# A gated recurrence in a fused four-layer kernel: head sums moved from VectorE, ScalarE and GpSimd to TensorE, with keys and values dealt to (token, head) partitions by DMA

## The chip, the cores and the metric

The kernel runs on one core of one Trainium2 chip. The metric is the device time of one execution in microseconds (us). The core has five instruction queues: PE (TensorE), DVE (VectorE), ACT (ScalarE), POOL (GpSimd) and SP (SyncE, here only an issuer of DMA transfers). They run side by side and are ordered only by semaphores that the program sets and waits for.

## The reference, cut to what matters

The program computes four residual layers over 8 sequences of 512 tokens with 256 channels. The change lies in the first, a gated recurrence followed by window attention. Of it, this part is touched (`n` sequence, `h` of 8 heads, `e` of 4 recurrences, `t` token, `d` of 64 channels; keys K and values V alike):

```python
G = sigmoid(einsum('ntd,hed->nhet', Xp, w_G) + b_G)
K = einsum('ntc,hdc->nhtd', Xp, w_K)
V = einsum('ntc,hdc->nhtd', Xp, w_V)
A = 1.0 - minimum(G.sum(axis=1), 1.0)
gK = einsum('nhet,nhtd->netd', G, K)
gV = einsum('nhet,nhtd->netd', G, V)
# tokens in 32 pieces of 16; in each piece, from the initial state iK (iV):
# Y[t] = A[t] * Y[t-1] + gK[t]
nK = _pscan(A, gK, iK);  nV = _pscan(A, gV, iV)
```

So each of 4096 tokens has 8 heads of 128 numbers (64 of K, 64 of V). For each `e` the heads are summed with the gates as factors, and the sums run through a linear scan along the tokens.

## The kernel before

The stage `recurrence` works in tiles of 128 tokens, 32 tiles, four to a sequence. Every engine runs one `stream` of steps: the first and last tiles written out, the rest in a hardware loop over sequences, so each engine has its own fixed order and stands still where a semaphore of its next instruction is missing. For a tile:

1. DVE normalises the rows (`normed`, tile `XN`), PE turns them (`turned`, `psT`), ACT copies them to `XT` (L452); SP stores `XT` to DRAM for the window attention (L349).
2. PE makes the gate logits `psG` (L400, L401), ACT takes the exponential (L457), DVE turns it into the gates `G` and the decays `A` in five small instructions (L519 to L529).
3. PE makes keys and values of all heads, tokens on partitions, in two PSUM banks (`psKV`, L409, four products of 512 columns).
4. The head sums are made with per-partition factors, one instruction for each (head, e) pair. Of the 32 pairs of a tile, DVE takes 20 (L542 the first head of an `e`, L545 the others, each adding to `acc`), ACT takes 12 (L470, into `gated`), and POOL adds ACT's twelve up in three instructions (L370, L372, L374).
5. PE turns the sums and the decays so that channels lie on partitions and tokens in a row (`psR`, L418 to L421; `psA`, L425), ACT copies them into `gT` and `AT` (L478, L480).
6. After the fourth tile of a sequence DVE adds the initial state at the first token of each piece of 16 and sets the decay there to zero (L556 to L558), and scans 512 tokens for each of the four `e` (L560), writing `Rec`.

DVE's order in a step: `normed` of the tile four ahead, the 20 pairs with the next tile's gate instructions in between, and, at the first step of a sequence, the scan of the sequence before. PE's order in a step: `turned` of the tile three ahead, gates of the tile two ahead, keys and values of the next tile, sums and decays of the last one. `psKV` has two buffers, so keys and values of a tile wait for the pairs of the tile two before.

The next stage, `window_attention`, starts behind a barrier of all engines, needs `Rec` and the first sequence of `XS`, loaded back from DRAM at the stage's end (L196). Instructions of other stages are not touched.

## Time and profile before

| | |
|---|---|
| median of 3 runs | 2017.03 us (2015.64 to 2017.1) |
| the profiled execution | 2017.16 us |
| its span, first to last instruction | 2015.4 us |
| mean granted TensorE clock | 0.918 |
| PE busy over the span | 1679.7 us (83%) |
| DVE busy over the span | 1211.6 us (60%) |
| ACT, POOL busy over the span | 664.2 us, 592.1 us |

The span is what the prediction works with, and the 1.8 us around it are taken as constant. Shares over the whole span say little here, since the change touches one stage, the first sixth of it. So the rows below are nearly all of that stage. In the rows, "PEld" is a weight load of PE, which runs beside the products. A product of float32 appears as two instructions (L409: 256 instructions for 128 products), a transpose as one. In a timeline a row may merge several neighbouring instructions of a kind (x4): its start is the first one's and its length reaches to the end of the last.

### The profile page before, as it was taken

What the parts mean: (1) busy time and instruction counts of PE and PEld (TensorE: products, weight loads), DVE (VectorE), ACT (ScalarE), POOL (GpSimd) and SP (SyncE); (2) the same over time, 40 slices, a digit from 0 to 9 for tenths busy, and PEclk for the clock granted to TensorE, in tenths of its full rate; (3) what the DMA queues carried; (4) which work ended last, traced back from release to release, by engine and by line L of the source; (5) the groups of instructions that cost most, each with busy time, mean ns of one, the idle gap of its engine ahead of it and who ended that gap; (6) DMA issues with size and microseconds to landing.
All of it is one profiled execution on the core that took longest, in us unless ns stands there. A gap on an engine that the chain in (4) does not pass through costs nothing. (4 is left out here: it accounts for less than half of the span.)

```text
span 2015.4 us, 33318 instructions
## 1 busy us (share of the span) xinstructions
PE 1679.7 (83%) x10092; PEld 1252.5 (62%) x10092; DVE 1211.6 (60%) x3206; ACT 664.2 (33%) x2056; POOL 592.1 (29%) x668
## 2 busy tenths in 40 slices
PE   4777765999899977367786999999599999699999
PEld 2444434777677754256675788888366666455655
DVE  5999994777677767599945122222388888422221
ACT  2545544555455533112230111111144444211121
POOL 2443432000000011587626332332354554100000
PEclk9898987999899998777775899999799999799999
DMA  6000000000000000000011232432210110000000
GB/s 187 17 16 13 16 21 11 12 11 12 13 12 12 1 9 0 6 0 22 21 67 70 86 110 89 94 104 62 94 30 29 31 31 17 1 11 21 10 21 21
DMA packets 55111, 71.08 MB, mean 35 GB/s; under 512 B 7074, under 2 KB 44898, under 8 KB 54626
## 3 DMA queue, kind: packets, MB, share of 16 engines
q1 hardware_dynamic: 37218, 40.46, 6.3%
q0 software_dynamic: 6912, 18.88, 3.6%
q10 hardware_dynamic: 10880, 10.49, 1.5%
q8 instruction: 51, 0.84, 0.2%
q14 instruction: 50, 0.41, 0.1%
HBM read 46.61 MB, written 23.20 MB: 35 GB/s over the span
## 5 line engine op out<-in xcount | busy, mean ns | idle before, releaser
L801 ACT ACTIVATE probs<-psS,nm 128x256 f32<-128x256 f32 x256 | 118.9, 469 | 191.9 <-DVE nm L834 191.9
L409 PE MATMUL psKV<-wkv,XT 128*128 128x512 f32 x256 | 135.4, 678 | 52.2 <-DVE acc L545 32.5
L1576 DVE COPY YE<-e_psY 128x512 f32<-128x512 f32 x40 | 27.6, 691 | 220.6 <-PE e_psY L1522 220.6
L545 DVE SCALAR_TENSOR_TENSOR acc<-psKV,G,acc 128x128 f32<-128x128 f32 x544 | 150.1, 332 | 6.7 <-ACT gated L470 6.7
L1512 PE MATMUL e_psH<-e_XT,w 128*128 128x256 f32 x640 | 147.3, 384 | 0.0
L1522 PE MATMUL e_psY<-w,e_HT 128*128 128x256 f32 x640 | 144.0, 379 | 0.0
L832 DVE TENSOR_REDUCE mx<-psS 128x2 f32<-128x512 f32 x128 | 87.8, 686 | 93.4 <-PE psS L722 93.4
L722 PE MATMUL psS<-Rec,QT 128*128 128x256 f32 (+1 forms) x512 | 134.4, 385 | 6.8 <-issue 5.9
L1482 POOL DMA_INDIRECT XE<-token_rows,held x80 | 76.0, 950 | 200.0 <-PE e_psX L1499 180.3
L1522 PEld LDWEIGHTS e_psY<-w,e_HT 128*128 128x128 f32 x640 | 121.6, 190 | 16.5
L1512 PEld LDWEIGHTS e_psH<-e_XT,w 128*128 128x128 f32 x640 | 120.7, 193 | 15.4
L1552 ACT ACTIVATE e_HT<-e_psH 128x512 f32<-128x512 f32 x80 | 47.8, 597 | 234.1 <-PE e_psH L1512 212.9
L409 PEld LDWEIGHTS psKV<-wkv,XT 128*128 128x128 f32 x256 | 52.6, 217 | 112.0 <-issue 94.6
L470 ACT ACTIVATE gated<-psKV,G 128x128 f32<-128x128 f32 x384 | 103.8, 407 | 36.0 <-DVE acc L545 18.3
L1104 PE MATMUL o_psA<-ident,prodV 128*128 128x128 f32 x400 | 61.6, 318 | 59.9 <-POOL prodV L1043 59.9
L722 PEld LDWEIGHTS psS<-Rec,QT 128*128 128x128 f32 x512 | 94.7, 192 | 21.5 <-issue 9.9
L2223 DVE SCALAR_TENSOR_TENSOR f_HT<-f_psU,f_SG 128x512 f32<-128x512 f32 x48 | 33.2, 692 | 124.2 <-PE f_psU L2155 111.1
L666 POOL COPY R<-Rec 128x2176 f32 (+1 forms) x8 | 16.0, 1997 | 289.1 <-PE psB L711 273.5
L1104 PEld LDWEIGHTS o_psA<-ident,prodV 128*128 128x128 f32 x400 | 57.5, 228 | 63.5 <-issue 42.7
L1038 POOL TENSOR_TENSOR prodS<-QKV 128x256 f32<-128x256 f32 (+1 forms) x104 | 83.4, 833 | 36.1 <-DVE sc L1191 18.6
L2151 PE MATMUL f_psG<-f_XT,wgu 128*128 128x512 f32 x192 | 92.1, 603 | 1.2 <-ACT f_XT L2183 1.2
L841 DVE TENSOR_SCALAR probs<-probs,rs 128x256 f32<-128x256 f32 x256 | 88.7, 389 | 4.9 <-DVE rs L838 0.4
(254 smaller groups left out, 3816.0 us busy)
## 6 DMA issues: line engine op xcount, KB each, us to landing
expert_out<-YE ACTq DMA_DIRECT2D x40, 256.0 KB, 2.2
w<-in_w SPq DMA_DIRECT2D x16, 512.0 KB
X<-in_x SPq DMA_DIRECT2D x8, 512.0 KB, 7.4
x_turned<-XT SPq DMA_DIRECT2D x32, 128.0 KB, 2.1
XS<-x_turned SPq DMA_DIRECT2D x8, 512.0 KB, 3.9
token_rows<-o_XN SPq DMA_DIRECT2D x32, 128.0 KB, 1.7
out_x<-X SPq DMA_DIRECT2D x8, 512.0 KB, 2.9
QT<-in_sel SPq DMA_DIRECT2D x2, 1024.0 KB, 11.7
```

Of the source, the lines that this page charges most:

```text
L409: mm = pe.matmul(psKV[v % 2][half][:, :, :], XT[:, v, c, :], wkv[:, c, half * 512:(half + 1) * 512], start=(c == 0), stop=(c == KC - 1))
L470: ins = nc.scalar.activation(gated[:, v % 2, place, :], psKV[v % 2][half][:, h % 4, :], ACT.Copy, scale=G[:, v, h * E0 + e:h * E0 + e + 1])
L545: ins = nc.vector.scalar_tensor_tensor(acc[:, v % 2, e, :], kv, g, acc[:, v % 2, e, :], ALU.mult, ALU.add)
L722: mm = pe.matmul(psS[b.q % 2][:, hg, :], QT[b.r][:, hg, b.q, :, :].rearrange("d h t -> d (h t)"), k.Rec[:, bass.ds(b.t, 1), b.q * QB:b.q * ...
L801: nc.scalar.activation(probs[:, b.q % 4, hg, :], psS[b.q % 2][:, hg, :], ACT.Exp, bias=nm[:, b.q % 2, hg:hg + 1], scale=scale, accum_out=s ...
L832: nc.vector.tensor_reduce(mx[:, b.q % 2, :], psS[b.q % 2][:, :, :], AX.X, ALU.max).then_inc(mx_done, 1)
L841: ins = nc.vector.tensor_scalar(probs[:, b.q % 4, hg, :], probs[:, b.q % 4, hg, :], rs[:, b.q % 2, hg:hg + 1], None, ALU.mult)
L1038: return eng.tensor_tensor(fwd(dst), q, bc(kk, [P, NKV, QG, HD]), ALU.mult)
L1104: mm = pe.matmul(psA[s % 2][:, c, :], src[:, t - t0, c * P:(c + 1) * P], k.ident[:, :], start=(t == 0 and c == 0), stop=(t == s and c == K ...
L1512: mm = pe.matmul(psH[c % 2][half][:, m, :], w1[:, s, kc, f:f + P], XT[:, c % 2, kc, :], start=(m == 0 and kc == 0), stop=(m == 1 and kc == ...
L1522: mm = pe.matmul(psY[c % 2][:, j, :], HT[:, c % 2, m, j * P:(j + 1) * P], w2[:, s, m, :], start=(j == 0 and m == 0), stop=(j == 1 and m == ...
L2151: mm = pe.matmul(psG[m % 2][:, :], wgu[:, c, m * P:(m + 1) * P], XT[:, c, :], start=(c == 0), stop=(c == KC - 1))
```

## The change

The head sums are now products on PE, summed over partitions. ACT copies the keys and values of a tile to SBUF as they are (`KV`, 8 heads of 132 numbers for each token, the last four being that head's gates, which DVE's reciprocal writes there). SP then deals them out: 8 DMAs for each tile (`deal`), each of which takes 16 tokens (16 partitions, 8 heads each) to 128 partitions of `KD`, one for each (token, head). POOL multiplies a constant 0/1 table `own` (a partition's token among the 16) with the dealt gates into `GB` (`spread`, 512 numbers for each partition). Eight products `KD` x `GB` with 64 columns each (`sums`) give the gated sums, already with channels on partitions and tokens in a row, in PSUM (`psC`). DVE adds the seed there and scans 128 tokens for each `e` straight out of PSUM, tile by tile. POOL makes the seed and zeroes the decays at the pieces' first tokens (`opened_at`). ACT's copy of the decays clamps at zero (Relu) in place of the minimum. `deal` waits for the keys and values and gates of its tile, and for the `sums` of the tile two before, which free `KD`. The same DMA completion (`dealt`) frees `KV` for ACT and for DVE's reciprocal two tiles later. SP now has the whole stage written out, no loop. `psKV` has one buffer for each half.

The diff, cut to its core (lines of before whose code stands above are left out where they are only removed):

```diff
+        self.own = k.sb(ctx, "own", [P, P // H0])
...
+        sp.dma_start(self.own[:, :], a["own"]).then_inc(self.loaded, 16)
...
-    HH = H0 // 2
-    EV = E0 - 1
-    summed_pairs = [(h, e) for h in range(H0) for e in range(EV if h < HH else EV - 1)]
-    NV = len(summed_pairs)
+    ROW = P + E0
+    GT = P // H0
+    NG = P // GT
...
-        eg = k.sb(ctx, "eg", [P, TS, HE])
-        G = k.sb(ctx, "G", [P, TS, HE])
-        A = k.sb(ctx, "A", [P, TS, E0])
-        gated = k.sb(ctx, "gated", [P, 2, H0 + HH, P])
-        acc = k.sb(ctx, "acc", [P, 2, E0 + 1, P])
-        gT = k.sb(ctx, "gT", [P, E0, T])
-        AT = k.sb(ctx, "AT", [P, E0, T])
-        seed = k.sb(ctx, "seed", [P, E0, L0])
-        psT = k.ps(ctx, "psT", [P, KC, P])
-        psG = k.ps(ctx, "psG", [P, TS, HE])
-        psKV = [[k.ps(ctx, f"psKV{s}{h}", [P, 4, P]) for h in range(2)] for s in range(2)]
-        psR = k.ps(ctx, "psR", [P, E0, P])
+        eg = k.sb(ctx, "eg", [P, 2, HE])
+        A = k.sb(ctx, "A", [P, 2, E0])
+        KV = k.sb(ctx, "KV", [P, 2, H0, ROW])
+        KD = k.sb(ctx, "KD", [P, 2, NG, ROW])
+        GB = k.sb(ctx, "GB", [P, 2, NG, E0, GT])
+        AT = k.sb(ctx, "AT", [P, 2, E0, P])
+        seed = k.sb(ctx, "seed", [P, 2, E0, NG])
+        psT = k.ps(ctx, "psT", [P, 2, KC, P])[:, 0, :, :]
+        psG = k.ps(ctx, "psG", [P, 4 * P])[:, 0:HE]
+        psKV = [k.ps(ctx, f"psKV{h}", [P, 4, P]) for h in range(2)]
+        psC = [k.ps(ctx, f"psC{x}", [P, E0, P]) for x in range(2)]
...
+            for t in range(-2, TS):
+                peeled(t)
...
+        class Tile:
+            def __init__(self, i, s, lag):
+                w = s + lag
+                self.t, self.i, self.u, self.x = i * TS + w, i + w // TS, w % TS, w % 2
+                self.pair = i * (TS // 2) + w // 2
+        def firsts(x):
+            return x.rearrange("p e (l c) -> p e l c", c=GT)[:, :, :, 0]
...
-            sp.wait_ge(zero_set, 1)
-            sp.dma_start(k.y_dram[SLOTS:SLOTS + P, :], zero[:, :]).then_inc(zero_stored, 16)
-            with sp.Fori(0, NB) as i:
-                for u in range(TS):
-                    sp.wait_ge(t_evac, i * TS + u + 2)
-                    sp.dma_start(k.xT_dram[:, :, bass.ds(i * T + u * P, P)], XT[:, u, :, :]).then_inc(xt_stored[u], 16)
+            def stored(c):
+                sp.wait_ge(t_evac, c.t + 1)
+                sp.dma_start(k.xT_dram[:, :, bass.ds(c.i * T + c.u * P, P)], XT[:, c.u, :, :]).then_inc(xt_stored[c.u], 16)
+            def deal(c):
+                sp.wait_ge(kv_evac, c.t * 2 + 2 + 2)
+                sp.wait_ge(g_gate, c.t + 1 + 1)
+                sp.wait_ge(c_ready, c.t + 1)
+                for g in range(NG):
+                    sp.dma_start(KD[:, c.x, g, :], KV[g * GT:(g + 1) * GT, c.x, :, :]).then_inc(dealt[c.x], 16)
+            def step(i, s, has):
+                if has(1):
+                    stored(Tile(i, s, 1))
+                if has(0):
+                    deal(Tile(i, s, 0))
+            for t in range(-1, NT):
+                step(t // TS, t % TS, lambda d: t + d < NT and t + d >= 0)
...
+            def spread(c):
+                pool.wait_ge(dealt[c.x], c.pair * (16 * NG) + 16 * NG)
+                pool.wait_ge(c_ready, c.t + 1)
+                nc.gpsimd.tensor_tensor(GB[:, c.x, :, :, :], bc(own[:, :].unsqueeze(1).unsqueeze(1), [P, NG, E0, GT]),
+                                        bc(KD[:, c.x, :, P:].unsqueeze(3), [P, NG, E0, GT]), ALU.mult).then_inc(gb_made, 1)
+            def opened_at(c):
+                pool.wait_ge(at_evac, c.t + 1 + 1)
+                pool.wait_ge(scan_done, c.t + 1)
+                nc.gpsimd.tensor_tensor(seed[:, c.x, :, :], firsts(AT[:, c.x, :, :]), ikv[:, :, c.u * NG:(c.u + 1) * NG],
+                                        ALU.mult).then_inc(seeded, 1)
+                pool.wait_ge(seeded, c.t + 1)
+                none = zero[:, 0:E0 * NG].rearrange("p (e l) -> p e l", e=E0)
+                nc.gpsimd.tensor_tensor(firsts(AT[:, c.x, :, :]), none, none, ALU.mult).then_inc(opened, 1)
+            def step(i, s, has):
+                if has(-1):
+                    spread(Tile(i, s, -1))
                 if has(0):
-                    head_sum(i * TS + u, u)
+                    opened_at(Tile(i, s, 0))
...
+            def keys_values(c):
+                pe.wait_ge(t_evac, c.t + 1)
                 for half in range(2):
+                    pe.wait_ge(kv_evac, c.t * 2 + half + 1)
+                    for h in range(KC):
+                        mm = pe.matmul(psKV[half][:, :, :], XT[:, c.u, h, :], wkv[:, h, half * 512:(half + 1) * 512],
+                                       start=(h == 0), stop=(h == KC - 1))
+                    mm.then_inc(kv_ready, 1)
+            def sums(c):
+                pe.wait_ge(gb_made, c.t + 1)
+                pe.wait_ge(scan_done, c.t + 1)
+                for g in range(NG):
+                    mm = pe.matmul(psC[c.x][:, :, g * GT:(g + 1) * GT], KD[:, c.x, g, 0:P],
+                                   GB[:, c.x, g, :, :].rearrange("p e t -> p (e t)"), start=(g == 0), stop=(g == NG - 1),
+                                   skip_group_check=True)
+                mm.then_inc(c_ready, 1)
+            def decays_turned(c):
+                pe.wait_ge(a_made, c.t + 1)
+                pe.wait_ge(at_evac, c.t + 1)
                 for e in range(E0):
+                    mm = pe.transpose(psA[:, e, :], bc(A[:, c.x, e:e + 1], [P, P]), k.ident[:, :])
+                mm.then_inc(a_ready, 1)
+            def step(i, s, has):
+                if has(0):
+                    keys_values(Tile(i, s, 0))
                 if has(1):
+                    turned(Tile(i, s, 1))
+                if has(-2):
+                    sums(Tile(i, s, -2))
+                if has(1):
+                    gates(Tile(i, s, 1))
+                if has(0):
+                    decays_turned(Tile(i, s, 0))
...
+            def kept(c, half):
+                if half == 0 and not (isinstance(c.t, int) and c.t < 2):
+                    act.wait_ge(dealt[c.x], c.pair * (16 * NG))
+                act.wait_ge(kv_ready, c.t * 2 + half + 1)
+                nc.scalar.copy(KV[:, c.x, half * 4:half * 4 + 4, 0:P], psKV[half][:, :, :]).then_inc(kv_evac, 1)
+            def turned(c):
+                act.wait_ge(t_ready, c.t + 1)
+                act.wait_ge(xt_stored[c.u], c.i * 16 + 16)
+                nc.scalar.copy(XT[:, c.u, :, :], psT).then_inc(t_evac, 1)
+            def exponential(c):
+                act.wait_ge(g_ready, c.t + 1)
+                act.wait_ge(g_gate, c.t)
+                nc.scalar.activation(eg[:, c.x, :], psG, ACT.Exp, scale=-1.0).then_inc(g_exp, 1)
+            def decays(c):
+                act.wait_ge(a_ready, c.t + 1)
+                act.wait_ge(scan_done, c.t + 1)
+                nc.scalar.activation(AT[:, c.x, :, :], psA[:, :, :], ACT.Relu).then_inc(at_evac, 1)
+            def step(i, s, has):
                 if has(0):
+                    kept(Tile(i, s, 0), 0)
+                    kept(Tile(i, s, 0), 1)
+                if has(1):
+                    turned(Tile(i, s, 1))
+                    exponential(Tile(i, s, 1))
                 if has(0):
+                    decays(Tile(i, s, 0))
...
+            def gates(c):
+                gate = KV[:, c.x, :, P:]
+                dve.wait_ge(g_exp, c.t + 1 + 1)
+                nc.vector.tensor_scalar(eg[:, c.x, :], eg[:, c.x, :], 1.0, None, ALU.add).then_inc(gate_step, 1)
+                if not (isinstance(c.t, int) and c.t < 2):
+                    dve.wait_ge(dealt[c.x], c.pair * (16 * NG))
+                dve.wait_ge(gate_step, c.t * 3 + 1)
+                nc.vector.reciprocal(gate, eg[:, c.x, :].rearrange("p (h e) -> p h e", e=E0)).then_inc(g_gate, 1)
+                dve.wait_ge(g_gate, c.t + 1 + 1)
+                dve.wait_ge(a_ready, c.t) if not (isinstance(c.t, int) and c.t == 0) else None
+                nc.vector.tensor_reduce(A[:, c.x, :], gate.rearrange("p h e -> p e h"), AX.X, ALU.add).then_inc(gate_step, 1)
+                dve.wait_ge(gate_step, c.t * 3 + 2)
+                nc.vector.tensor_scalar(A[:, c.x, :], A[:, c.x, :], -1.0, 1.0, ALU.mult, ALU.add).then_inc(a_made, 1)
+                dve.sem_inc(gate_step, 1)
+            def scan(c):
+                dve.wait_ge(c_ready, c.t + 1 + 2)
+                dve.wait_ge(opened, c.t + 1)
+                nc.vector.tensor_tensor(firsts(psC[c.x][:, :, :]), firsts(psC[c.x][:, :, :]), seed[:, c.x, :, :],
+                                        ALU.add).then_inc(scan_step, 1)
+                dve.wait_ge(scan_step, c.t + 1)
                 for e in range(E0):
+                    out = k.Rec[:, bass.ds(c.i, 1), L0 + c.u * P:L0 + (c.u + 1) * P, e].rearrange("p a t -> p (a t)")
+                    scan = nc.vector.tensor_tensor_scan(out, AT[:, c.x, e, :], psC[c.x][:, e, :], 0.0, ALU.mult, ALU.add)
+                scan.then_inc(scan_done, 1)
+            def step(i, s, has):
                 if has(0):
+                    gates(Tile(i, s, 0))
+                if has(2):
+                    normed(Tile(i, s, 2))
+                if has(-2):
+                    scan(Tile(i, s, -2))
```

PE's order in a middle step of the stage's loop. Before (`psR` are the sums turned, `psA` the decays, `psKV` keys and values):

```order
L418 MATMUL psR<-ident,acc 128x128 x3
L420 MATMUL psR<-ident,acc 128x128
L421 MATMUL psR<-ident,acc 128x128
L422 REGISTER_ALU
L425 MATMUL psA<-ident,A 128x128 x4
L390 REGISTER_ALU
L393 MATMUL psT<-ident,XN 128x128 x2
L400 MATMUL psG<-wg,XT 128x32 x2
L401 MATMUL psG<-bg,ones 128x32
L405 ISA
L406 ISA
L409 MATMUL psKV<-wkv,XT 128x512 x4
```

Now, in the last steps (written out, so without register instructions):

```order
L443 MATMUL psKV<-wkv,XT 128x512 x4
L428 MATMUL psT<-ident,XN 128x128 x2
L452 MATMUL psC<-GB,KD 128x4x16 x8
L435 MATMUL psG<-wg,XT 128x32 x2
L436 MATMUL psG<-bg,ones 128x32
L462 MATMUL psA<-ident,A 128x128 x4
```

The five instructions of `psR` (two of them products) are gone, eight products `psC` of 64 columns are new, and stand behind the keys and values of the tile two later and ahead of the next tile's gates.

SP's queue in the stage, before: one store for each tile, in a loop.

```order
L348 REGISTER_ALU
L349 ISA
L349 DMA x_turned<-XT 256x1x128
```

And now, at its start; the last two rows repeat for the rest of the stage:

```order
L194 DMA QT<-in_sel 64x4096 x2
L358 DMA x_turned<-XT 256x1x128 x2
L366 DMA KD<-KV 128x1x132 x8
L358 DMA x_turned<-XT 256x1x128
L366 DMA KD<-KV 128x1x132 x8
```

The queue gets eight more DMAs for each tile, each store stands between two deals, and the load of `XS` behind the last deal.

DVE in a middle step of the loop, now:

```order
L537 TENSOR_SCALAR eg<-eg 128x32
L540 ISA
L541 RECIPROCAL KV<-eg 128x8x4
L544 TENSOR_REDUCE A<-KV 128x4
L545 REGISTER_ALU
L546 TENSOR_SCALAR A<-A 128x4
L278 ISA
L278 TENSOR_SCALAR XN<-X,mean,rstd 128x256
L552 TENSOR_TENSOR psC<-psC,seed 128x32
L557 ISA
L557 SCALAR_TENSOR_TENSOR Rec<-AT,psC 128x128
L557 ISA
```

The 20 instructions on (head, e) pairs are gone from DVE. The scan (the row named SCALAR_TENSOR_TENSOR with `Rec`, four in all) comes every tile, last in the step.

## Rows read from the trace of the kernel before

**Rows 1.** Stretches: length, PE, PEld, DVE, ACT, POOL busy us; granted clock, DMA share, GB/s.
```profile
36.00:310.00 274.00, 198.59 (x818) 117.28 (x817) 254.12 (x870) 142.68 (x499) 112.77 (x93) 0.90 0.06 17
...
310.00:327.00 17.00, 4.87 (x22) 4.09 (x20) 5.88 (x9) 3.38 (x8) 3.25 (x3) 0.50 0.00 0
```

**Rows 2.** Groups of instructions to 440 us: count, busy us, mean ns, idle before.
```profile
L545 DVE SCALAR_TENSOR_TENSOR acc<-psKV,G,acc 128x128 f32<-128x128 f32 x544 | 150.1, 332 | 6.7 <-ACT gated L470 6.7
L409 PE MATMUL psKV<-wkv,XT 128*128 128x512 f32 x256 | 135.4, 678 | 52.2 <-DVE acc L545 32.5 <-ACT gated L470 17.5 <-DVE acc L542 1.8
L560 DVE TENSOR_TENSOR_SCAN Rec<-AT,gT 128x512 f32 (+1 forms) x32 | 53.7, 1738 | 1.1 <-DVE AT L558 1.0
...
L370 POOL TENSOR_TENSOR gated<-gated 128x512 f32<-128x512 f32 x32 | 40.6, 1269 | 162.8 <-ACT gated L470 162.8
...
L557 DVE TENSOR_TENSOR gT<-gT,seed 128x128 f32<-128x128 f32 x8 | 3.0, 378 | 0.3
...
L480 ACT COPY AT<-psA 128x512 f32<-128x512 f32 x32 | 18.9, 591 | 0.5 <-PE psA L425 0.5
```

**Rows 3.** Timeline of PE, one tile in the written-out part.
```profile
45.24 0.49 PE L418 MATMUL psR<-ident,acc 128*128 128x128 f32 x3
45.57 0.39 PE L420 MATMUL psR<-ident,acc 128*128 128x128 f32 x2
...
46.02 0.60 PE L425 MATMUL psA<-ident,A 128*128 128x128 f32 x4
46.45 0.38 PE L393 MATMUL psT<-ident,XN 128*128 128x128 f32 x2
46.67 0.53 PE L400 MATMUL psG<-wg,XT 128*128 128x32 f32 x4
47.13 0.40 PE L401 MATMUL psG<-bg,ones 1*128 1x32 f32 x2
```

**Rows 4.** Timeline of PE and its weight loads: three keys-and-values blocks, one gates block.
```profile
29.52 6.38 PE L409 MATMUL psKV<-wkv,XT 128*128 128x512 f32 x8
...
41.73 3.67 PE L409 MATMUL psKV<-wkv,XT 128*128 128x512 f32 x8 [0.37 <-issue]
...
46.56 0.53 PEld L400 LDWEIGHTS psG<-wg,XT 128*128 128x128 f32 x4
47.13 0.29 PEld L401 LDWEIGHTS psG<-bg,ones 1*128 1x128 f32 x2
...
81.98 5.75 PE L409 MATMUL psKV<-wkv,XT 128*128 128x512 f32 x8 [3.69 <-DVE acc L545]
```

**Rows 5.** Timeline around the fourth-tile scan, and at the stage's end.
```profile
213.50 7.00 DVE L560 TENSOR_TENSOR_SCAN Rec<-AT,gT 128x512 f32 x4 [0.17 <-DVE AT L558]
...
214.65 2.06 POOL L372 TENSOR_TENSOR gated<-gated 128x512 f32<-128x512 f32 x1
...
317.53 0.87 PE L418 MATMUL psR<-ident,acc 128*128 128x128 f32 x3 [5.25 <-POOL acc L374]
...
321.93 4.57 DVE L560 TENSOR_TENSOR_SCAN Rec<-AT,gT 128x512 f32<-128x512 f32 x4
```

**Rows 6.** DMA issues by SP: start, length of the issue (of several, to the last's end).
```profile
0.76 7.11 SPq L213 DMA_DIRECT2D X<-in_x  x8
...
1054.25 0.47 SPq L1612 DMA_DIRECT2D rotC<-in_rotC  x1
1054.76 0.44 SPq L1612 DMA_DIRECT2D rotS<-in_rotS  x1
```

**Rows 7.** One source line each (L349, then L213): issue ns, and time to landing.
```profile
L349 SPq DMA_DIRECT2D x_turned<-XT x32: 541/542/677, 29.3 to 280.6; - x32
...
DMA to landing us min/median/max: 2.1/2.1/8.2
...
DMA to landing us min/median/max: 4.1/7.4/8.9
```

**Rows 8.** DMA queues from 60 to 280 us: packets, MB, share of 16 engines.
```profile
q1 hardware_dynamic: 6528, 3.15, 4.9%
```

More of the change, by code:

```diff
@@ L383, in _ @@
         def _(pe):
-            pe.sem_inc(t_ready, 2)
-            pe.sem_inc(kv_ready, 4)
-            pe.sem_inc(ra_ready, 8)
-            pe.wait_ge(weights, 64)
-            def turned(t, v):
-                pe.wait_ge(t_evac, t + 1)
-                pe.wait_ge(xn_ready, t + 1)
-                for c in range(KC):
-                    mm = pe.transpose(psT[:, c, :], XN[:, v % 2, c * P:(c + 1) * P], k.ident[:, :])
-                mm.then_inc(t_ready, 1)
-            def gates(t, v):
-                pe.wait_ge(t_evac, t + 2)
-                pe.wait_ge(g_exp, t + 1)
-                for c in range(KC):
-                    pe.matmul(psG[:, v, :], XT[:, v, c, :], wg[:, c, :], start=(c == 0), stop=False)
-                pe.matmul(psG[:, v, :], k.ones[0:1, :], bg[0:1, :], start=False, stop=True).then_inc(g_ready, 1)
@@ L403, in keys_values @@
-            def keys_values(t, v):
-                pe.wait_ge(t_evac, t + 2)
-                pe.wait_ge(acc_step, t * NV + NV)
-                pe.wait_ge(gated_ready, t * 2 + 6)
-                for half in range(2):
-                    for c in range(KC):
-                        mm = pe.matmul(psKV[v % 2][half][:, :, :], XT[:, v, c, :],
-                                       wkv[:, c, half * 512:(half + 1) * 512], start=(c == 0), stop=(c == KC - 1))
-                mm.then_inc(kv_ready, 1)
@@ L428, in step @@
-            def step(i, u, has):
-                g = i * TS + u
-                if has(3):
-                    turned(g + 3, (u + 3) % TS)
-                if has(2):
-                    gates(g + 2, (u + 2) % TS)
-                if has(1):
-                    keys_values(g + 1, (u + 1) % TS)
-                if has(-1):
-                    sums_turned(g - 1, (u - 1) % TS)
+            pe.sem_inc(c_ready, 2)
+            pe.wait_ge(weights, 80)
+            def turned(c):
+                pe.wait_ge(xn_ready, c.t + 1)
+                pe.wait_ge(t_evac, c.t)
+                for h in range(KC):
+                    mm = pe.transpose(psT[:, h, :], XN[:, c.x, h * P:(h + 1) * P], k.ident[:, :])
+                mm.then_inc(t_ready, 1)
@@ L459, in gate @@
-            def gate(t, v, half):
-                if half == 1:
-                    act.wait_ge(kv_ready, t + 1 + 4)
-                    act.wait_ge(g_gate, t + 1 + 4)
-                    act.wait_ge(gated_summed, t + 1)
-                else:
-                    act.wait_ge(acc_step, t * NV + (HH * EV + 2 * NV))
-                for h in range(4 * half, 4 * half + 4):
-                    for e in (EV, EV - 1)[:1 + half]:
-                        place = h if e == EV else h + HH
-                        ins = nc.scalar.activation(gated[:, v % 2, place, :], psKV[v % 2][half][:, h % 4, :], ACT.Copy,
-                                                   scale=G[:, v, h * E0 + e:h * E0 + e + 1])
-                ins.then_inc(gated_ready, 1)
@@ L474, in sums_turned @@
[L474 to L491 removed]
+            act.sem_inc(kv_evac, 2)
@@ L564, in step @@
-            def step(i, u, has):
-                g = i * TS + u
-                if isinstance(g, int) and g == 0:
-                    rows.ready(dve, 1)
-                if has(4):
-                    normed(g + 4, u)
-                if has(0):
-                    head_sum(g, u, has(1))
-                elif has(1):
-                    for part in range(GATE_PARTS):
-                        gates(g + 1, (u + 1) % TS, part)
-                if u == 0 and has(-1):
-                    scan(i - 1)
+            dve.wait_ge(weights, 80)
@@ new lines, in normed, with gates @@
+            def normed(c):
+                if isinstance(c.t, int) and c.t == TS:
+                    rows.ready(dve, 1)
+                if not (isinstance(c.t, int) and c.t < 2):
+                    dve.wait_ge(t_ready, c.t - 1)
+                normalise(k, XN[:, c.x, :], c.t).then_inc(xn_ready, 1)
+            def gates(c):
+                gate = KV[:, c.x, :, P:]
+                dve.wait_ge(g_exp, c.t + 1 + 1)
+                nc.vector.tensor_scalar(eg[:, c.x, :], eg[:, c.x, :], 1.0, None, ALU.add).then_inc(gate_step, 1)
+                if not (isinstance(c.t, int) and c.t < 2):
+                    dve.wait_ge(dealt[c.x], c.pair * (16 * NG))
[7 more added lines that the diff above has]
+                dve.sem_inc(gate_step, 1)
@@ L2277, in lay_out @@
     c["before"] = np.triu(np.ones((P, P), np.float32), 1)
+    c["own"] = f(np.kron(np.eye(P // H0, dtype=np.float32), np.ones((H0, 1), np.float32)))
     c["iota"] = f(np.tile(np.arange(P, dtype=np.float32), (P, 1)))
```

145 lines of the change are left out of this document (26 added, 119 removed).

## The prediction, made before the changed kernel ran

> **What bounds the kernel now.** I read the busy time by stretch first. From 36 to 310 us DVE is busy 254 of 274 us, PE 199, ACT 143, POOL 113 [rows 1]. So the stage is DVE's. The groups say with what: 544 pair instructions L545 of 332 ns and 32 scans of 1738 ns [rows 2]. PE's keys and values waited 52 us, 34 of them for DVE's `acc` and 17.5 for ACT's `gated` [rows 2]: consumers of `psKV` that had not freed it. The stage ends with the last scan, 321.93 + 4.57 = 326.5 us [rows 5]. From the first keys and values at 29.52 us [rows 4] that is 297 us, 9.3 us for each of 32 tiles. Anything that takes the pairs off DVE must be judged by what comes next, and that is PE.
>
> **PE's cost of a tile, from starts in the timeline.** Keys and values 41.73 to 45.24: 3.51 us. Decays turned 46.02 to 46.45: 0.43. Turned rows 0.22. Gates 0.46, bias 0.29 (its weight loads) [rows 3, 4]. Together 4.91 us; all of it stays. Removed are the turned sums, 45.24 to 46.02: 0.78 us. New are eight products, 16 instructions, each with a full 128x128 float32 weight load and 64 columns. The trace has none with 64. From below: L420 and L421, four instructions with 128 columns, 45.57 to 46.02, 0.11 each: 1.8 us. From above: the four weight loads of L400, 46.56 to 47.13, 0.1425 each: 2.3 us [rows 3, 4]. I take 2.3, as L400 too has few columns behind a full load. Period of a tile if PE never waits: 4.91 + 2.3 = 7.2 us (6.7 with the lower bound).
>
> **Do the others keep up with 7.2 us?**
> - DVE: all that is neither L545 nor a scan is 254.1 - 150.1 - 53.7 = 50 us, 1.6 a tile, and some of that goes too [rows 1, 2]. The scan is now 128 numbers, four a tile. Four scans of 512 took 7.00 us with POOL at work and 4.57 with POOL idle [rows 5], so a tile's share is 1.1 to 1.75 us. The seed's addition is below 0.38 (L557) [rows 2]. DVE: under 3.8.
> - ACT: five instructions, none larger than L480's 0.59 [rows 2]: under 3.0.
> - POOL: `spread` has 512 numbers like L370's 1.27 and L372's 2.06 beside a scan [rows 2, 5]; I take 1.5. Two instructions of 32 numbers cost less than 1.27 each. Under 4.6.
> - SP: eight more issues. Plain ones follow each other every 0.5 us (1054.25, 1054.76) [rows 6]; eight are 4.0, and the store 0.54 [rows 7]: 4.5.
> - DMA engines: 6528 packets took 4.9% of 16 engines over 220 us, 26 ns each [rows 8]. A deal has 1024 pieces of 528 bytes: 1.7 us for each tile over 16 engines.
>
> **The chain through a deal.** Count from the start of PE's step t. Keys and values end at 3.5, turned rows at 3.7, `sums` of tile t-2 at 6.0. ACT has copied the second half by 4.4. So `deal`(t) starts when `sums`(t-2) free `KD`, at about 6.1. Issue 4.0 and landing 2.1 [rows 7] make D = 6.1: landed at 12.2, `spread` done at 13.8. `sums`(t) stand in PE's queue at 2 x 7.2 + 3.7 = 18.1. There are 4 us to spare. Behind SP's waiting `deal` stands the next store, due at 4.9 of the next step, when SP has been free since 2.9. DVE scans tile t-2 from 6.2 to at most 8.4, then makes the gates of t+1, whose logits came at 7.2. ACT's copy of the decays waits for that scan, so it ends at 9.0, 1.8 us into the next step; the first half of keys and values is ready for ACT just then. That is the tightest place outside PE, and costs nothing while the scans stay at 2 us.
>
> **Ends.** At the start PE runs at half pace, 6.38 us for the first keys and values against 3.67 [rows 4]. They now wait for one turned tile and one gates block, no longer for three and two, at that pace 2 x (0.44 + 0.75) = 2.4 us less: 27.1. Step 0 takes 6.4 and then 2 x 1.2 at mixed pace: step 1 at 35.9. It has no `sums` yet: step 2 at 40.8. Step 31 at 40.8 + 29 x 7.2 = 249.6. There everything is in the open: `sums`(29) end at 5.8, deal from 6.0 to 12.1, `spread` to 13.7, `sums`(31) 2.3 us at the slow pace after a wait (L418 took 0.87 us against 0.49 [rows 3, 5], factor 1.7) 3.9, seed and scans 2.3: 19.9 us. The load of `XS` now stands behind the last deal, at 260, and hides under those last 9 us: a plain store or load landed after at most 8.9 us, at the start under full load [rows 7]. Stage end: 249.6 + 19.9 = 269.5 against 326.5, **57 us less**. Nothing behind the barrier changes. 2017.2 - 57 = **1960 us** (the profiled execution agrees with the median within 0.2).
>
> **Two rules weighed.** The row: a store of 128 KB over 128 partitions lands after 2.1 us [rows 7]; none starts from 16 partitions only. The Trainium skill, "SBUF — State Buffer", section "Door 1: The DMA port swizzle", says that partitions 0 to 15 reach 4 of 16 ports and that a transfer on them got 104 GB/s; by it each 67.6 KB piece of a deal lasts 0.65 us, a deal 5.2 in place of 4.0. That would add some 1 us to the end and leave the period at 7.2; no row here shows it.
> The row: the scans took 7.00 us beside POOL and 4.57 without [rows 5]. The same page, section "Who interferes with whom", says that a VectorE instruction with two SBUF inputs and a reading GpSimd instruction exclude each other; the new scan reads one input from PSUM. By it the shares of 4.57 hold, 0.6 us less at the end; the trace agrees so far as the last scan, with POOL idle, is the short one.
>
> **Rivals.**
> - *SP or the DMAs set the pace.* For it: the eight X loads took 7.11 us to issue, 0.89 each [rows 6], and `deal` is always eight in a row. Against it: those had 512 KB each, these 68. With 0.89 a step costs SP 7.1 + 0.54 = 7.7, D = 9.2: end 60.7 + 29 x 7.7 + 3.1 = 287, **1978 us**. With landings of about 5 us instead of 2.1 as well (D = 12), the next rival's formula gives P = 8.2 and 1995.
> - *PE keeps falling to the lower clock.* After waits of 3.7 and 5.3 us PE was slow (5.75 us for keys and values) [rows 4, 5]; the granted clock averaged 0.90 [rows 1]. If steps still have such waits and it stays at 0.90 of full, P = 8.0: **1983 us**. Against it: no wait above 1 us is left in a step by the sum above.
> - *The round of a deal is longer than two steps: slower than before.* `KD` has two buffers, so 2P is at least D + `spread` 1.5 + `sums` 2.3 + semaphores 0.6 = D + 4.4. It sets the pace from D = 10. The whole stage is 60.7 (40.8 + 19.9) + 29P + (D - 6.1) and reaches 326.5 at P = 8.9, D = 13.5. Issue 7.1 and the longest X landing 8.9 give D = 16, P = 10.2, end 366: **2057 us**. Against it: a deal moves 0.54 MB, those eight 4.2 MB.
> - *No change*: only at that crossing, by chance.
>
> **How the numbers follow.** PE-paced as summed 0.62 (own range 1946, with P = 6.7, to 1972); SP or DMA pace 0.17 (to 1995); clock 0.10; deal round, slower 0.09; same 0.02. The range 1943 to 1992 leaves out the slower rival, the worst of the first, and a PE below 1.8 us for `sums`. 0.2% (4 us) is what three runs that spread over 1.5 us can tell. Faster 0.89, same 0.02, slower 0.09.
>
> **What would show it.** Right: starts of two neighbouring keys-and-values blocks 6.7 to 7.4 us apart, PE over 90% busy in the stage at a clock near 1, `sums` 1.8 to 2.3 us, DVE under 3.8 of each step, `KD` landings about 2 us after issue, last scan at 262 to 278 us. Wrong: PE's `psC` row waiting for POOL's `GB`, with POOL behind the DMA `KD` (deal round); SP issues of `KD` at 0.8 us or more without a wait (SP's pace); a clock near 0.9 or below with keys and values over 5 us in mid-stage. A start of window attention that waits for `XS` would mean that the end is not hidden.

## The result: 1937.18 us, 3.8% less, and the profile after

The median fell from 2016.34 to 1937.18 us (four runs each); the ratio is 0.9621, 95% interval 0.9607 to 0.9634. The prediction was 1960 with a range from 1943: right in its sign, and too high by more than its range allowed. The profiled execution, from which the lines below come, took 1934.66 us.

The busy time by stretch, of the kernel after, in the middle of the recurrence and at its end (columns as in [rows 1]):

```profile
40.00:240.00 200.00, 200.00 (x1068) 138.76 (x1067) 82.69 (x293) 66.64 (x149) 47.81 (x90) 1.00 0.61 101
240.00:256.00 16.00, 7.64 (x50) 7.10 (x50) 4.66 (x15) 0.86 (x2) 2.61 (x4) 0.69 0.44 86
```

PE works in 200.00 of 200.00 us at a granted clock of 1.00, its upper level. VectorE is down from 254 of 274 us [rows 1] to 83 of 200. DMA is busy 0.61 of the time, ten times as much as before. One step in the timelines of the kernel after (start, length, engine, line):

```profile
205.87 0.38 PE L428 MATMUL psT<-ident,XN 128*128 128x128 f32 x2
206.09 1.90 PE L452 MATMUL psC<-GB,KD 128*128 128x64 f32 x16
207.82 0.58 PE L435 MATMUL psG<-wg,XT 128*128 128x32 f32 x4
...
209.15 3.60 PE L443 MATMUL psKV<-wkv,XT 128*128 128x512 f32 x8
...
215.88 3.60 PE L443 MATMUL psKV<-wkv,XT 128*128 128x512 f32 x8
...
208.07 5.05 SPq L366 DMA_DIRECT2D KD<-KV  x8
...
208.33 1.05 POOL L398 TENSOR_TENSOR GB<-own,KD 128x512 f32<-128x512 f32 x1 [3.98 <-DMA KD<-KV]
...
208.39 1.35 DVE L557 TENSOR_TENSOR_SCAN Rec<-AT,psC 128x128 f32 x4 [0.17 <-DVE psC L552]
```

The period is 215.88 - 209.15 = 6.73 us, with no wait on PE. `sums` start at 206.09 and the next group at 207.82: 1.73 us, or 0.108 for each of 16 instructions. POOL waits 3.98 us for each deal and VectorE for PE, and neither costs anything, since PE waits for neither of them: `GB` made at 216.1 is used at 219.5.

The stage's end, PE:

```profile
243.41 2.00 PE L452 MATMUL psC<-GB,KD 128*128 128x64 f32 x16 [1.60 <-POOL GB L398]
249.50 3.68 PE L452 MATMUL psC<-GB,KD 128*128 128x64 f32 x16 [4.09 <-POOL GB L398]
255.85 1.62 PE L696 MATMUL psB<-XS,wq 128*128 128x256 f32 x3 [2.67 <-ACTq L768]
```

Here the last deal is in the open, and the last `sums` run at half pace behind a wait. The window attention's first product starts at 255.85; before, at 327.55. So the recurrence gave 71.7 us. In the window attention behind it, whose instructions are the same, one of PE's groups on the page differs. Its row of before, then that of after (the last part is idle time ahead of the group and its cause; "issue" is time in which PE waited for nothing that the profile shows):

```profile
L722 PE MATMUL psS<-Rec,QT 128*128 128x256 f32 (+1 forms) x512 | 134.4, 385 | 6.8 <-issue 5.9
```

```profile
L712 PE MATMUL psS<-Rec,QT 128*128 128x256 f32 (+1 forms) x512 | 132.3, 381 | 0.9 <-ACT QT L779 0.9
```

That stage took 420.18 us before and 411.04 after (from its first product to the load of the following stage's weights). 71.7 + 9.1 = 80.8 of the 82.6 us between the two spans; 1.8 are spread over the rest.

### The profile page after: what moved, and what is told of

Same layout as the page of the kernel before. It is cut to its first block and busy times, and to the rows that moved or that the text cites. A ratio compares the mean times of both kernels' runs of the same rounds, so it can differ in the third digit from the quotient of the medians.

```text
span 1932.8 us, 32628 instructions
## 1 busy us (share of the span) xinstructions
PE 1677.7 (87%) x10380; PEld 1271.0 (66%) x10380; DVE 1041.2 (54%) x2638; ACT 588.2 (30%) x1704; POOL 527.4 (27%) x668
## 5 line engine op out<-in xcount | busy, mean ns | idle before, releaser
L443 PE MATMUL psKV<-wkv,XT 128*128 128x512 f32 x256 | 117.1, 601 | 0.0
L2145 PE MATMUL f_psU<-f_XT,wgu 128*128 128x512 f32 x192 | 90.5, 594 | 0.0
L838 DVE COPY PT<-psP 128x512 f32<-128x512 f32 x128 | 87.4, 683 | 0.9 <-PE psP L722 0.9
L2154 PE MATMUL f_psY<-wd,f_HT 128*128 128x256 f32 x384 | 85.0, 381 | 1.8 <-issue 0.8
```

Source lines behind the costliest of these rows:

```text
L443: mm = pe.matmul(psKV[half][:, :, :], XT[:, c.u, h, :], wkv[:, h, half * 512:(half + 1) * 512], start=(h == 0), stop=(h == KC - 1))
L838: nc.vector.tensor_copy(PT[:, b.q % 2, :, :, :], psP[b.q % 2][:, :, :, :]).then_inc(p_evac, 1)
L2145: mm = pe.matmul(psU[m % 2][:, :], wgu[:, c, FF + m * P:FF + (m + 1) * P], XT[:, c, :], start=(c == 0), stop=(c == KC - 1))
L2154: mm = pe.matmul(psY[u % 2][:, :], HT[:, m, u * P:(u + 1) * P], wd[:, m, :], start=(m == 0), stop=(m == M - 1))
```

## The experiments

### Does PE set the new pace, and what do the products cost?

**All eight products twice.** All eight run a second time over the first, so PE does the work twice and the sums stay the same.

```diff
-                for g in range(NG):
+                for g in [*range(NG), *range(NG)]:
```

> The eight products of `sums` run twice for each tile, the second set over the first; all else stays and the result is the same. In the changed kernel the steps are 6.72 us apart, and `sums` are 1.73 us of that. Theory (PE sets the step, everything else has slack): step 8.45 us, 32 x 1.73 = 55 us more, about 1992 us. Rival (the round of a deal or the chain DVE - ACT sets it, PE only looks busy): part of the added time falls into existing waits, under 30 us more.

1995.25 us, ratio 0.9891 (0.9875 to 0.9908). The steps are 8.51 us apart, 1.79 more, and PE is busy 249.99 of 250.00 us. 58 us more than the changed kernel: what PE gets to do in a step is added to the period in full. The theory that PE sets the pace holds.

**Each product cut into two of 32 columns** (nothing left out, 32 instructions instead of 16).

```diff
-                    mm = pe.matmul(psC[c.x][:, :, ...], KD[...], GB[:, c.x, g, :, :], ...)
+                    for q in range(2):
+                        mm = pe.matmul(psC[c.x][:, 2 * q:2 * q + 2, ...], KD[...], GB[:, c.x, g, 2 * q:2 * q + 2, :], ...)
...
```

> The same sums as 16 products of 32 columns in place of 8 of 64; result unchanged. It measures the price that the prediction mis-sized. If an instruction costs what its full weight load costs (0.108 us as in the changed kernel's 64-column products), `sums` take 3.5 us and the kernel about 1992 us. If few columns are dearer (0.1425 each, the gate products' price that the prediction took), `sums` take 4.6 us, the step is 9.5 us, about 2027 us.

2040.86 us in its one execution, over both branches. Timeline of PE and stretches of that kernel:

```profile
202.13 5.08 PE L443 MATMUL psKV<-wkv,XT 128*128 128x512 f32 x8
207.06 0.38 PE L428 MATMUL psT<-ident,XN 128*128 128x128 f32 x2
207.28 3.66 PE L453 MATMUL psC<-GB,KD 128*128 128x32 f32 x32
210.77 0.61 PE L435 MATMUL psG<-wg,XT 128*128 128x32 f32 x4
```

```profile
201.90:204.90 3.00, 3.00 (x7) 1.45 (x6) 1.83 (x7) 0.60 (x1) 0.51 (x2) 0.50 0.62 91
204.90:207.00 2.10, 2.10 (x6) 0.85 (x5) 0.00 (x0) 0.59 (x1) 0.00 (x0) 0.95 0.73 107
207.00:210.70 3.70, 3.70 (x35) 3.64 (x33) 0.00 (x0) 0.86 (x2) 1.06 (x1) 1.00 0.23 50
```

An instruction of 32 columns takes 3.49 / 32 = 0.109 us, as one of 64 does (0.108), so between these two widths the count of instructions is the price. Their own price, 1.76 us more, would give steps of 8.5 us, like those of the run before. But the keys and values behind them ran at a granted clock of 0.50, the lower level, for 3 us, without PE having waited: 5.08 us instead of 3.60. What PE did before was the run of narrow products; that they are the cause is likely, but only this one execution shows it. From the tenth step on the steps were 10.0 to 10.2 us: 1.8 us from the price and about 1.7 from the clock.

**Half of the contraction of keys and values left out**, so that PE has 1.8 us less to do:

```diff
-                    for h in range(KC):
+                    for h in range(1):
...
```

> Keys and values are made from the first 128 of 256 channels only (half of their products left out, so the values are not the reference's). PE's step would fall by 1.76 to 4.96 us. If PE is the only floor: 31 x 1.76 = 55 us less, 1882 us. If SP's queue is the next floor (eight issues 5.05 + store 0.58 + small gaps = 5.7 us): 31 x 1.0 = 31 us less, about 1905 us. If the round of a deal is it (7.0 from first issue to GpSimd's start, 1.15, `sums` 1.73, release 0.25, over two steps = 5.1): about 1887 us.

1911.64 us, ratio 0.9484 (0.9468 to 0.9500), nearest to the branch with SP's queue. The mean step is 6.03 us, uneven. SP's queue and the busy time by stretch of that kernel:

```profile
150.14 5.06 SPq L366 DMA_DIRECT2D KD<-KV  x8
155.25 0.61 SPq L358 DMA_DIRECT2D x_turned<-XT  x1
155.96 5.05 SPq L366 DMA_DIRECT2D KD<-KV  x8
161.06 0.60 SPq L358 DMA_DIRECT2D x_turned<-XT  x1
```

```profile
50.00:210.00 160.00, 149.11 (x868) 111.16 (x866) 79.17 (x271) 58.67 (x136) 40.76 (x81) 0.95 0.68 113
```

SP goes from one deal straight to the store and the next deal: 155.96 - 150.14 = 5.8 us for each tile. Between 50 and 210 us it waited 1.5 us in all, and the last twenty steps of PE are 5.85 us in the mean. That is the floor under the changed kernel, 0.9 us below its pace.

**The deal in 16 DMAs of 33 KB instead of 8 of 66 KB**, same bytes:

```diff
-                    sp.dma_start(KD[:, c.x, g, :], KV[g * GT:(g + 1) * GT, c.x, :, :]).then_inc(dealt[c.x], 16)
+                    for q in range(2):
+                        sp.dma_start(KD[q * 64:(q + 1) * 64, c.x, g, :],
+                                     KV[g * GT + q * 8:g * GT + q * 8 + 8, c.x, :, :]).then_inc(dealt[c.x], 16)
...
```

> Each of the 8 transfers of a deal is cut into two of 64 destination partitions: 16 issues for each tile, same bytes, result unchanged. Rival of the prediction (SP or the deal round sets the pace) made real: at 0.63 us an issue SP needs 16 x 0.63 + 0.58 = 10.7 us a step, 4 us more than PE, 31 x 4.0 = 123 us more, about 2060 us, slower than the kernel before. If a half-size transfer issues in 0.5 us: 8.6 us a step, about 1995 us. If the deal had enough slack to hide it: no change.

2079.19 us, ratio 1.0314 (1.0297 to 1.0331): slower than before the change. Busy time by stretch, the group of `sums` between 60 and 235 us, and the issues (ns: least, median, most) of that kernel:

```profile
50.00:350.00 300.00, 243.57 (x979) 165.74 (x979) 80.25 (x270) 58.65 (x135) 41.03 (x81) 0.80 0.38 61
...
L454 PE MATMUL psC<-GB,KD 128*128 128x64 f32 x256 | 40.8, 326 | 34.2 <-POOL GB L400 34.2
...
L367 SPq DMA_DIRECT2D KD<-KV x512: 604/605/867, 34.6 to 388.9; - x171
```

PE waits for `GB`, its clock averages 0.80, steps are 10.9 us apart in the mean. SP's queue in that kernel:

```profile
146.21 10.32 SPq L367 DMA_DIRECT2D KD<-KV  x16
156.57 0.59 SPq L358 DMA_DIRECT2D x_turned<-XT  x1
157.27 10.31 SPq L367 DMA_DIRECT2D KD<-KV  x16
```

SP never stands still: 157.27 - 146.21 = 11.06 us a tile. So this is the prediction's first rival, SP's pace, made real. Its sign "`psC` waiting for `GB`, with POOL behind the DMA", which was meant for the round of a deal, comes with SP's pace as well. An issue of 33 KB costs 605 ns where one of 66 KB costs 599 (the changed kernel's median). So the number of DMAs set the pace here, and halving the bytes of each gave nothing back. But a half also reads from 8 partitions instead of 16, and a source whose speed goes by its partitions would take as long for it. This run doesn't tell the two reasons apart.

### What was the 9 us in a stage that nobody touched?

**The kernel before once more, unchanged.**

> The kernel before, unchanged, profiled once more. Beyond the stage of the change the changed kernel's window attention was 9.1 us shorter (from the first PE instruction of that stage to the first load of the next: 420.2 against 411.0 us); in before's trace PE stood 5.08 us for `issue` at the end of that stage's hardware loop, and then ran slow for some us. If that wait belongs to this program's code as laid out, it is there again with about 5 us and the stage takes 420 us. If it is chance of one execution, it is gone or another size.

2014.32 us in one execution; window attention 417.98 us, `psS` again with 4.9 us of "issue" (two waits, 3.57 and 1.31).

**The kernel before with 32 idle semaphore increments at the head of PE's queue in the recurrence.**

```diff
+            for _ in range(32):
+                pe.sem_inc(k.gates_passed, 1)
```

> The kernel before with 32 semaphore increments more at the start of PE's queue in the recurrence, where PE waits for the first rows anyway; they shift all of PE's later code by 32 instructions. Theory (the 5 us wait at the loop's end hangs on where PE's code lies when it is fetched): the wait changes size and window attention takes 411 to 416 us in place of 420; the kernel 4 to 9 us faster. Rival (the shorter window attention comes from how the recurrence leaves it, an engine's state or the clock): it stays at 420 us, no change.

2008.38 us, ratio 0.9967 (0.9953 to 0.9980). Window attention takes 411.3 us, the recurrence's last scan ends at 327.45, 0.9 later than before. PE where the window attention's hardware loop ends, in the kernel before and with the increments:

```profile
541.97 1.64 PE L722 MATMUL psS<-Rec,QT 128*128 x3 [5.08 <-issue]
544.45 0.80 PE L722 MATMUL psS<-Rec,QT 128*128 x1 [0.84 <-issue]
```

```profile
L724 PE MATMUL psS<-Rec,QT 128*128 128x256 f32 (+1 forms) x512 | 132.3, 381 | 0.9 <-ACT QT L791 0.9
```

32 instructions that do nothing take away the wait of 5.9 us and the slow products behind it. The traces of all variants tell the same: nine of the kernel before without the increments have a wait of 3.4 to 5.3 us there and a stage of 417.6 to 420.5 us, the seven of the changed kernel and its variants have none and 410.4 to 411.1. So this part of the gain belongs to where the code lies in PE's queue, not to what the recurrence does. Which code position makes PE wait there, and for what, no run here shows.

### What did the change take out of the recurrence?

The prediction said: VectorE's work. Seven kernels, all variants of the kernel before.

**Four of VectorE's twenty pairs of a tile left out** (`e` = 2 of heads 0 to 3), then **four of ScalarE's twelve** (`e` = 2 of heads 4 to 7), then **both**; what is left out stands as zeros:

```diff
-    summed_pairs = [(h, e) for h in range(H0) for e in range(EV if h < HH else EV - 1)]
+    summed_pairs = [(h, e) for h in range(H0) for e in range(2)]
...
-                    for e in (EV, EV - 1)[:1 + half]:
+                    for e in (EV,):
```

> The kernel before with 4 of DVE's 20 (head, e) pairs left out (e = 2 of heads 0 to 3; that part of the sums is zero). Theory (DVE sets the pace of the stage before): 4 x 0.332 x 32 = 42 us less at most, 25 or more, as ACT's 12 pairs of 0.407 and its copies stand close behind at 143 of 274 us. Rival (the exchange between PE and the two buffers of `psKV`, or the stall at each scan, is the pace): under 12 us less.

> The kernel before with 8 instead of 12 of the scaled value channels on ScalarE in each tile (channel 2 of heads 4 to 7 is left out and stands as zeros, so GpSimd still adds it). Theory one (an ordinary step of 6.9 us is set by two chains that end almost together, the products and their scaling on ScalarE, and VectorE's own work, as the run without four of VectorE's pairs showed no gain): less than 10 us less, ordinary steps of 6.6 to 6.9. Theory two (the chain through ScalarE alone sets an ordinary step): 4 instructions of about 0.3 us less in each of 24 ordinary steps, 25 us or more, steps below 6.

> Both cuts in one: the kernel before without four of VectorE's twenty pairs and without four of ScalarE's twelve in each tile (channel 2 of all eight heads is left out). Theory one (two chains that end almost together): only now the ordinary step falls, to 5.7 to 6.1 us, and the time by 25 to 35 us. Theory two (something else sets the step, the matrix products or GpSimd): less than 10 us, steps of 6.6 to 6.9. The step of the scan keeps its 12 to 13 us by both.

2012.94 us (ratio 0.9995, 0.9986 to 1.0005), 2015.56 (0.9991, 0.9974 to 1.0008) and 2014.45 (0.9999, 0.9990 to 1.0008): nothing, three times, with ordinary steps of the loop of 6.85 to 7.1 us each time. (Ordinary are those other than the one that holds the scan, below called the stall step, and the one behind it.) My theory of two chains that end almost together falls with the third. PE's own timeline in the kernel before, and ScalarE's beside it, name the real one:

```profile
98.05 3.70 PE L409 MATMUL psKV<-wkv,XT 128*128 128x512 f32 x8 [0.85 <-ACT gated L470]
101.72 0.55 PE L418 MATMUL psR<-ident,acc 128*128 128x128 f32 x3
...
102.32 0.39 PE L421 MATMUL psR<-ident,acc 128*128 128x128 f32 x2
...
104.91 3.70 PE L409 MATMUL psKV<-wkv,XT 128*128 128x512 f32 x8 [0.85 <-ACT gated L470]
...
102.74 0.58 ACT L478 COPY gT<-psR 128x512 f32<-128x512 f32 x1 [2.32 <-PE psR L421]
103.22 0.59 ACT L480 COPY AT<-psA 128x512 f32<-128x512 f32 x1
103.70 3.22 ACT L470 ACTIVATE gated<-psKV,G 128x128 f32<-128x128 f32 x12
```

The next keys and values wait for the first four of those twelve `gated`, which free a buffer of `psKV`; ScalarE makes them behind two copies, and the first copy waits for the turned sums, which stand in PE's queue behind the keys and values. 3.67 + 1.02 + 0.96 + 1.21 = 6.86 us, a ring. None of the instructions left out lies on it: of `gated`, only the second half's were.

**The order of that ring changed**: ScalarE makes the first half's `gated` ahead of the two copies. Nothing is left out. Once so, and once together with the four pairs of VectorE left out:

```diff
-                if has(-1):
-                    sums_turned(g - 1, (u - 1) % TS, i)
                 if has(0):
                     gate(g, u, 0)
+                if has(-1):
+                    sums_turned(g - 1, (u - 1) % TS, i)
```

> The kernel before with one change of order on ScalarE: its four products of the first half of the heads stand ahead of the two copies of the turned head sums instead of behind them; nothing is left out. Theory (the chain keys-and-values 3.70, transposes 1.02, two copies 0.97, four products 1.21, together 6.9 us, sets an ordinary step, with VectorE's 6.6 us of work next): ordinary steps of 6.5 to 6.7 us, 3 to 8 us less. Rival one (VectorE sets the step after all): 6.85 and no change. Rival two (the copies now come later and TensorE's transposes wait for them): steps over 6.9, slower.

> The same change of order together with four of VectorE's twenty pairs left out (channel 2 of heads 0 to 3 stands as zeros), which alone changed nothing. Theory (chain through ScalarE first, VectorE next): ordinary steps fall to 5.6 to 6.1 us, 15 to 25 us less. Rival (neither of the two sets the step, but something else of 6.9 us): no step below 6.6, less than 8 us.

1990.20 us (ratio 0.9882, 0.9864 to 0.9900) and 1982.66 (0.9844, 0.9826 to 0.9861). Both gained more than I expected, 24 us where I had said 3 to 8, and 32 where I had said 15 to 25. Ordinary steps of the loop with the new order are 5.76 to 6.82 us, and with fewer pairs mostly 5.76. One step of the first of the two, by stretch:

```profile
92.76:99.00 6.24, 5.86 (x29) 3.75 (x28) 6.24 (x26) 4.40 (x16) 2.21 (x3) 1.00 0.07 21
```

Only here is VectorE the bound: 6.24 of 6.24 us, and 194 of 199 us over the loop's 24 steps, where it was 198 of 216 in the kernel before. So the ring through ScalarE set an ordinary step before, and VectorE stood 0.6 us behind it.

**The scan shortened** to the first 128 of 512 positions, and **left out**:

```diff
...
-                for e in range(E0):
-                    n = nc.vector.tensor_tensor_scan(k.Rec[:, bass.ds(i, 1), L0:WIN, e]..., AT[:, e, :], gT[:, e, :], ...)
-                n.then_inc(scan_done, 1)
+                dve.sem_inc(scan_done, 1)
```

> The kernel before, whose scan at the end of each sequence's fourth tile covers only the first 128 of the 512 positions for each of the four channels (the rest of the recurrence's result is left out and stands as zeros). In the kernel before, the steps of the recurrence are about 6.9 us apart, but once in each sequence one of 13.28 us stands behind the scan of 7.00 us, and the next takes 8.1 to 9.4. Theory one (this stall is what the change removed, while its ordinary steps cost hardly less): the stall step shrinks to 7.5 to 8.5 us and the one behind it to about 7, together 7 to 8 us in each of seven sequences, and 3.4 to 5 us at the end: 50 to 60 us less, a time near 1960. Theory two (the head sums leaving the other engines is what gave the gain, and the scan's time is merely moved): less than 20 us, with the stall step still over 11.

> The kernel before without the scan's four instructions (the recurrence's result is left out and stands as zeros; the three small instructions ahead of it stay). Theory (the scan and what it holds up is nearly all that the change removed from the recurrence; its ordinary steps of 6.9 us became 6.72): the stall step falls by the scan's 7.01 us, from 13.28 to 6.3 to 7.5 us, the step behind it from 8.1 to 9.4 to about 7, so 8 to 9.5 us in each of seven sequences, and 4.6 at the end: 60 to 70 us less, a time of 1945 to 1955. Rival (the block behind the stall is slow for another reason than the wait): the step behind stays at 8 to 9.7 and the gain is 47 to 53 us.

1988.26 us (ratio 0.9871, 0.9855 to 0.9887), between both theories, and 1963.45 (0.9755, 0.9728 to 0.9781). The stall step of each sequence was 13.28 us in the kernel before and 10.17 with the short scan, less by 3.11, as the scan itself is (7.00 to 3.89). I had expected about 1.4 for it, since 128 numbers take that when nothing else runs. Without the scan that step is 7.31 us, the steps are 7.16 in the mean, and the window attention starts at 275.05, 52.5 us earlier. The number is the rival's, but its reason is not: the step behind the stall did become short (7.10), and what is missing to 60 us is mainly one step of about 9.36 in each eight, in which keys and values took 5.39 us:

```profile
96.06 5.39 PE L410 MATMUL psKV<-wkv,XT 128*128 128x512 f32 x8 [1.29 <-DVE acc L546]
```

### A version that beats both

**The gate's bias multiplied in after the exponential** (exp(-x-b) = exp(-x) exp(-b); VectorE multiplies, PE's L436, one product a tile, goes), and then also **the last tile's deal issued half by SyncE, half by ScalarE**. Nothing is left out.

```diff
-                pe.matmul(psG, k.ones[0:1, :], bg[0:1, :], start=False, stop=True).then_inc(g_ready, 1)
+                nc.vector.tensor_tensor(eg[:, c.x, :], eg[:, c.x, :], EB[:, :], ALU.mult).then_inc(bias_step, 1)
...
-                for g in range(NG):
+                for g in range(NG // 2 if c.t == NT - 1 else NG):
+                    for g in range(NG // 2, NG):
+                        act.dma_start(KD[:, c.x, g, :], KV[g * GT:(g + 1) * GT, c.x, :, :]).then_inc(dealt[c.x], 16)
```

> The changed kernel without the product that adds the gate bias for each tile: exp(-b) is made once on the chip and DVE multiplies it in (0.2 us more on DVE, which waits 3.6 us in each step). PE's step falls by 0.33 to 6.39 us: 31 x 0.33 = 10 us less, about 1927 us, if PE's queue is all that counts; no change if a chain around PE has that slack.

> The changed kernel with the gate's bias taken out of the per-tile product and multiplied into the exponential by VectorE instead, and the last tile's deal issued half by SyncE and half by ScalarE. Theory (the last tile's deal is exposed, since nothing follows it that could hide its 5.05 us of issues): about 2.4 us less than the version with the bias alone (1919), near 1917. Rival (the two queues' issues or transfers get in each other's way, or the sums of the last tile wait for something else): no difference to that version.

1919.11 us (ratio to before 0.9531, 0.9516 to 0.9545), with steps of 6.27 us: 0.45 less for a group whose starts lay 0.34 apart (L436 to L462), so its removal also closed a gap. And 1918.12 (0.9524, 0.9509 to 0.9539). The intervals overlap, so the time doesn't tell these two apart. In the traces the end, from the last keys and values to the window attention, is 17.75 us instead of 19.85, as the theory had it, while the start of the stage came out 0.4 us later.

## Why the prediction was off, by its own steps

- **"New are eight products ... I take 2.3"**: the larger of two steps that failed, by a term mis-sized. 1.73 us measured, just under the lower bound of 1.8. The price of an instruction was that of L420 and L421 (0.11). The 0.1425 was a misreading: it divides 46.56 to 47.13 by four, but the four loads of L400 end 0.53 us after 46.56 [rows 4], and the median load of that line lasts 0.19, so they start (0.53 - 0.19) / 3 = 0.11 apart too. What is left up to 47.13 is a gap ahead of the bias's load. The period came out at 6.72 instead of 7.2 (the lower bound gave 6.7), and 29 x 0.48 = 13.9 us of the 14.7 by which the recurrence was forecast too long. The rest is in the ends: step 2 came at 41.10 instead of 40.8, and from step 31 at 236.04 to the last scan's end at 254.8 it took 18.8 us instead of 19.9.
- **"Nothing behind the barrier changes"**: failed too, 9.1 us, by the position of code in PE's queue. The run with 32 idle increments shows the size without the change. With `sums` priced right the forecast would have been 1960 - 13.9 = 1946 us, with this step alone right 1951. Either lies in the range; both together took the time below 1943.
- **"So the stage is DVE's"**: wrong as a cause, without harm to the sum, which was made from the new side. VectorE was busy 93% [rows 1], but in part with a scan that the others had to wait for. An ordinary step was the ring through ScalarE. Of the 71.7 us, taking the scan out of before alone gives 52.5. What is left, 19.2, is 13.2 in steps (7.16 against 6.73, 31 times), 3.8 at the end and 2.2 at the start. The changed kernel still scans; it does so in a VectorE that PE doesn't wait for.
- **"Eight are 4.0"**: 5.05, and **"1.7 us for each tile"** of DMA engines: q1's 37081 packets took 60.1% of 16 engines over 175 us, 45 ns each instead of 26.

```profile
q1 hardware_dynamic: 37081, 17.50, 60.1%
```

  A deal and a store are 1426 packets: 4.0 us of every 6.7. Both terms lay beside PE's work, and the 3.4 us to spare took them. Landings took 2.4 us, where 2.1 was assumed.
- **Door 1** (the Trainium skill, "SBUF — State Buffer", section "Door 1: The DMA port swizzle") gave an estimate of 5.2 for a deal, and the series of issues took 5.05. The 16 DMAs with half the bytes took 605 ns each just the same; but each read 8 neighbouring partitions, which by the same section of the Trainium skill reach 2 ports instead of 4, so its estimate for a half is 0.65 us too. Whether ports or a fixed price of an issue set these 0.6 us stays open.
- **"Who interferes with whom"** (the Trainium skill, same page) said that a scan with one input from PSUM doesn't exclude POOL. Scans of 4 x 128 numbers: 3.89 us beside POOL with both inputs in SBUF (the short scan), 1.37 without POOL (its last), and 1.35 beside POOL's L398, with `psC` from PSUM; L398 takes 1.05 beside the scan and 1.05 without it (the last one, at 248.40). The trace agrees, for both engines. Its timeline in the kernel with the short scan, middle and end:

```profile
101.66 3.89 DVE L561 TENSOR_TENSOR_SCAN Rec<-AT,gT 128x128 f32 x4 [0.17 <-DVE AT L559]
...
299.48 1.37 DVE L561 TENSOR_TENSOR_SCAN Rec<-AT,gT 128x128 f32<-128x128 f32 x4
```

- **The rivals.** SP's pace is real at 5.8 us and would set the pace if PE had 0.9 less to do. PE's clock stayed at 1.00. The deal round decided in no run: even with twice the issues it was SP's queue.
- **The signs.** Steps of 6.72 us, PE busy throughout at a clock of 1.00, 2.8 us of DVE in a step and `KD` landings of 2.4 us were as named. `sums` of 1.73 us and a last scan that ended at 254.8 lay below what was named.

## What to carry to other kernels

The busiest engine need not be the one that sets a step: write down from the timeline the ring of waits from one start of the repeated block to the next, and add it up, before calling a stage an engine's. Here one change of order on an engine that was 52% busy [rows 1] gave 24 us, a third of what the rewrite gave. Price a new instruction by its like in an unhindered row, and when a difference shows up in a stage that wasn't touched, move the code by some idle instructions before giving the change the credit.

## What the runs showed that I had not expected

- A run of 32 instructions with 32 columns each (16 products), without any wait, was followed by 3 us at a granted clock of 0.50 (one execution); 16 instructions of 64 columns (1.73 us), or 32 of them (3.5 us), were not (PE at 1.00 throughout).
- PE can lose 5 to 6 us (5.9 and 4.9 in two executions of the kernel before) at a hardware loop's end, and some more to the lower clock behind it (0.74 over 535 to 555 us, against 1.00 with the increments), by the position of its code alone.
- SBUF to SBUF, each of a series of DMAs takes 0.60 us to issue, and the next starts 0.64 us after it, whether it holds 66 KB from 16 partitions or 33 KB from 8. Those of 66 KB land 2.4 us after their issue. For those of 33 KB the trace has no landing, but `GB` starts 2.5 us after a deal's last issue in both kernels.
